# Third selective scan of a fused network kernel: units of 1024 columns on 64-row matmul tiles, with u overwritten in PSUM

## The reference

```python
def mamba_fwd(x, in_w, conv_w, conv_b, xproj_w, dt_w, dt_b, A_log, Dp, out_w):
    ...                                    # x: 4*B sequences of L = 1024, 16 channels
    xc = silu(conv(xi) + conv_b)           # di = 32 channels
    dbl = xc @ xproj_w.T                   # dt (4), B (16), C (16)
    dt = softplus(dtr @ dt_w.T + dt_b)
    A = -exp(A_log)
    def step(h, inp):
        dA = exp(dt_t[..., None] * A)
        h = dA * h + (dt_t * x_t)[..., None] * B_t[:, None, :]
        y = einsum('bds,bs->bd', h, C_t)   # 16 states
        return (h, y)
    y = ys + xc * Dp
```

## Time and profile before

| | us |
|---|---|
| median of 3 runs | 2011.63 (2010.33 to 2016.12) |
| the profiled execution | 2010.27 |
| its span in the trace | 2008.3 |
| scan3 in it, from its first instruction to its last | 1374.0 to 1904.9 |

### The profile page before, as it was taken

One profiled execution on the slowest core, in us unless ns is written; L12 is line 12 of the kernel. 1 busy time (PEld: TensorE's weight loads), 2 busy tenths in 40 slices (PEclk: granted clock), 3 DMA queues, 4 the chain that ended last, 5 costly groups with the idle time before them and its releaser, 6 DMA issues. The chain is left out here.

```text
span 2008.3 us, 31048 instructions
## 1 busy us (share of the span) xinstructions
PE 1594.7 (79%) x9878; PEld 876.8 (44%) x9878; DVE 1585.5 (79%) x1549; ACT 1164.7 (58%) x1889; POOL 1168.3 (58%) x881
## 2 busy tenths in 40 slices
PE   4888787996777877787777776667889888888787
PEld 2555434884333333333333333234555554454333
DVE  3788745554899999999999999441889999999854
ACT  3444484334666666676666665275656666665356
POOL 0666501001567676767767775202999999999701
PEclk8999988997899999899989998776999999999898
DMA  4000000000344444444444445100000000000001
GB/s 135 2 0 0 1 0 1 1 1 1 63 89 90 90 87 94 84 94 85 93 84 91 92 88 95 39 1 0 1 1 0 0 0 0 0 0 0 8 4 42
DMA packets 23435, 78.21 MB, mean 39 GB/s; under 512 B 3792, under 2 KB 4816, under 8 KB 23120
## 3 DMA queue, kind: packets, MB, share of 16 engines
q0 software_dynamic: 18432, 67.12, 17.7%
q1 hardware_dynamic: 4944, 10.35, 1.8%
HBM read 8.25 MB, written 2.10 MB: 5 GB/s over the span
## 5 line engine op out<-in xcount | busy, mean ns | idle before, releaser
L1177 POOL TENSOR_TENSOR s_prod<-s_ahead,s_cs 128x1024 f32<-128x1024 f32 x128 | 309.7, 2419 | 208.8 <-DVE s_back L1154 153.7
L1712 POOL TENSOR_TENSOR r_prod<-r_state,r_cs 128x512 f32<-128x512 f32 x256 | 323.7, 1316 | 15.7 <-DVE r_state L1653 15.1
L1151 DVE TENSOR_TENSOR_SCAN s_ahead<-s_fore,s_pfeed 128x1024 f32<-128x1024 f32 x128 | 292.7, 2287 | 10.4 <-ACT s_fore L1073 3.9
L1154 DVE TENSOR_TENSOR_SCAN s_back<-s_aft,s_pfeed 128x1024 f32<-128x1024 f32 x128 | 289.5, 2262 | 0.0
L1640 DVE TENSOR_TENSOR r_feed<-r_pu,r_bs 128x512 f32<-128x512 f32 x256 | 164.9, 689 | 64.2 <-PE r_pu L1482 64.2
L1073 ACT ACTIVATE s_fore<-s_pd,s_aneg 128x896 f32<-128x896 f32 x128 | 130.1, 1016 | 135.9 <-PE s_pd L942 135.2
L1144 DVE TENSOR_TENSOR s_pfeed<-s_pu,s_bs 128x1024 f32<-128x1024 f32 x128 | 157.8, 1233 | 35.4 <-PE s_pu L942 22.6
L1605 ACT ACTIVATE r_decay<-r_pd,r_aneg 128x512 f32<-128x512 f32 x256 | 168.7, 687 | 25.2 <-PE r_pd L1482 24.9
L942 PE MATMUL s_pu<-s_partsu,selr 64*128 64x512 f32 x512 | 102.2, 479 | 102.0 <-DVE s_pfeed L1144 102.0
L1482 PE MATMUL r_pu<-r_parts,selr 128*128 128x512 f32 x512 | 162.7, 440 | 5.7 <-DVE r_feed L1640 5.7
L1653 DVE TENSOR_TENSOR_SCAN r_state<-r_decay,r_carry,r_feed 128x512 f32<-128x512 f32 x128 | 156.5, 1267 | 0.0
(11 more groups left out here) (255 smaller groups left out, 3357.7 us busy)
## 6 DMA issues: line engine op xcount, KB each, us to landing
s_ahead<-s_back POOLq DMA_DIRECT2D x128, 512.0 KB, 4.5
x_act<-in_x_dram SPq DMA_DIRECT2D x8, 256.0 KB, 5.6
out_dram<-x_act SPq DMA_DIRECT2D x16, 128.0 KB, 2.3
k_scan<-in_pack_scan_dram SPq DMA_DIRECT2D x1, 1600.0 KB, 10.7
k_fir<-in_pack_fir_dram SPq DMA_DIRECT2D x1, 1600.0 KB, 14.0
k_l<-in_pack_l_dram SPq DMA_DIRECT2D x1, 450.0 KB, 7.1
k_ln<-in_pack_ln_dram SPq DMA_DIRECT2D x3, 131.0 KB, 2.6
k_mlp<-in_pack_mlp_dram SPq DMA_DIRECT2D x2, 194.0 KB, 5.1
```

What stands on the lines that cost most here:

```text
L1151: dve.tensor_tensor_scan(ahead[:, v % 4], f, feed[:], 0.0, ALU.mult, ALU.add).then_inc(ahead_done, 1)
L1154: dve.tensor_tensor_scan(back[:, v % 4, ::-1], a[:, ::-1], feed[:, ::-1], 0.0, ALU.mult, ALU.add).then_inc(back_done, 1)
L1177: pool.tensor_tensor(prod[:, b], ahead[:, v % 4], cs[:, buf].rearrange("p i n -> p (i n)"), ALU.mult).then_inc(prod_done, 1)
L1712: pool.tensor_tensor(prod[:, v % 2, q], state[:, v % 2, q], cs[:, v % UNROLL // 4, q], ALU.mult).then_inc(multiplied, 1)
```

## The change

`scan3` works in units: one (q, g) of 1024 columns, 128 in all, in a loop unrolled by 32 with 32 peeled ones at each end. A unit takes the place of two (q, g) of 512 columns, so the number of columns on each engine is the same.

- **u in place.** `ps_u` has two buffers of 1024 columns (two banks each), `ps_d` one, and the feed is written over `ps_u`. The separate feed banks are gone. DVE does feed, then the scan of the same unit.
- **64-row tiles.** The spread of u for one unit and of delta for the next one is one job of eight matmuls with 64 rows each, which alternate between the upper and the lower half of the array. PE waits for the scan of the unit before last, and for ACT's exp of the one before, ahead of it.
- **The scan** always starts at 0.0, as a unit holds whole sequences. The carry and its activation are gone.
- **POOL** multiplies in place in `state` (four buffers). It no longer makes `grown` (ACT does) nor the low part of B and C: PE subtracts the high part in PSUM (`negid`), and ACT copies the rest. It has six sums a group instead of eight.
- **y.** Dp * xc comes into `ps_y` by two fp32 matmuls with `place` ahead of each group of 8 units; DVE's L1669 is gone, and ACT copies `ps_y` to xc in four pieces of 32 rows.
- **First sums on VectorE.** For the first two groups, before any unit runs, the sums are DVE's (`EARLY`).
- The constants grow by `place` (512 columns) and `negid` (128), and DVE makes two tiles from them at the start.

```diff
-           ("alog", 4), ("dp", 1)],
+           ("alog", 4), ("dp", 1), ("place", 4 * P), ("negid", P)],
...
+UNROLL3, PEEL3 = 32, 32
...
-        ps_d, ps_u, feed = m.banks("r_pd", 2), m.banks("r_pu", 2), m.banks("r_feed", 2)
+        decay, state = (m.sb("r_" + t, [P, 4, 2 * N]) for t in ("decay", "state"))
+        bs, cs = (m.sb("r_" + t, [P, 2, 2, 2 * N]) for t in ("bs", "cs"))
+        ps_d, ps_u = m.banks("r_pd", 1, (P, 2 * N))[0], m.banks("r_pu", 2, (P, 2 * N))
+        ps_m, ps_y = (m.banks("r_p" + t, 1)[0] for t in "my")
...
-        LAG_B, LAG_D, LAG_U, LAG_Y = 2, 5, 6, 7
+        LAG_B, LAG_E, LAG_D, LAG_A, LAG_P, LAG_Y, LAG_V = 12, 16, 17, 18, 19, 20, 21
+        EARLY = 16
...
+        def cells(u):
+            u %= UNROLL3
+            half, phase = u // 16, u % 16 // 8
+            return half, phase, phase + u % 2 * 2, u % 8 // 2
...
         @block.tensor
+                if live(p, UNITS):              # p = s - LAG_D
+                    if (u - LAG_D) % 16 == 0:
+                        pe.wait_ge(lo_u, p + 16)
+                    wait(pe, scanned, p - 1)
+                    jobs.append((ps_u[(u - LAG_D) % 2], parts_u[:, half], q, g, u_rep))
+                if live(e, UNITS):              # e = s - LAG_E
+                    if (u - LAG_E) % 16 == 0:
+                        pe.wait_ge(lo_d, e + 16)
+                    wait(pe, decayed, e)
+                    jobs.append((ps_d, parts_d[:, half], q, g, d_ps))
+                for chunk in range(2):
+                    for part in range(2):
+                        for bank, parts, q, g, done in jobs:
+                            rows, at = slice(q // 2 * 64, q // 2 * 64 + 64), slice(chunk * N, (chunk + 1) * N)
+                            mm = pe.matmul(bank[:, at], selr[rows, (4 * q + g) * P:(4 * q + g + 1) * P],
+                                           parts[rows, part, at], start=(part == 0), stop=(part == 1),
+                                           tile_position=(q // 2 * 64, 0))
...
+                if k == 2 and live(s, UNITS):
+                    pe.wait_ge(hi_bc, gi + 8)
+                    pe.matmul(ps_m[:], negid[:], parts_bc[:, par, 0, at], start=False, stop=True,
+                              skip_group_check=True).then_inc(bc_rest, 8)
...                                             # then one spread of B or C, after s_copied, relu_done or lo_bc
+                if z % 2 == 1 and live(o, UNITS):    # o = s - LAG_Y, z = o mod 32
+                    if z % 8 == 1:
+                        wait(pe, y_done, o - 1)
+                        for chunk in range(2):
+                            pe.matmul(ps_y[:], place[:, 2 * phase + chunk],
+                                      xc[:, columns(o - z % 16 + 8 * chunk, N)], start=(chunk == 0), stop=False,
+                                      skip_group_check=True)
+                    pe.wait_ge(multiplied, o + 1)
+                    for chunk in range(2):
+                        for q in (phase, phase + 2):
+                            quad = q ^ chunk
+                            mm = pe.matmul(ps_y[quad * 32:(quad + 1) * 32], ysel[:, g * 32:(g + 1) * 32],
+                                           state[:, (z - 1 + q // 2) % 4, chunk * N:(chunk + 1) * N], start=False,
+                                           stop=(g == 3), tile_position=(0, quad * 32), skip_group_check=True)
+                    mm.then_inc(y_part, 2)
...                                             # k = 0: wdt, k = 1: wbc, both after s_copied
         @block.scalar
+                    act.wait_ge(d_ps, e + 1)
+                    wait(act, scanned, e - 3)
+                    act.activation(decay[:, v % 4], ps_d[:], ACT.Exp, scale=aneg[:, g:g + 1]).then_inc(decayed, 1)
...
+                if z % 8 == 7 and live(o, UNITS):    # o = s - LAG_V
+                    act.wait_ge(y_part, o + 1)
+                    for chunk in range(2):
+                        for q in (phase, phase + 2):
+                            rows, src = slice(q * 32, q * 32 + 32), (q ^ chunk) * 32
+                            done = act.activation(xc[rows, columns(o - z % 16 + 8 * chunk, N)], ps_y[src:src + 32],
+                                                  ACT.Copy)
+                    done.then_inc(y_done, 8)
...
         @block.vector
+                    dve.wait_ge(u_rep, p + 1)        # p = s - LAG_A
+                    if v % 8 < 2:
+                        dve.wait_ge(s_copied, p + 2 + v % 8)
+                    feed = ps_u[v % 2]
+                    dve.tensor_tensor(feed[:], feed[:], bs[:, phase, q // 2], ALU.mult).then_inc(fed, 1)
+                    dve.wait_ge(fed, p + 1)
+                    dve.wait_ge(decayed, p + 1)
+                    wait(dve, y_part, p - 3)
+                    dve.tensor_tensor_scan(state[:, v % 4], decay[:, v % 4], feed[:], 0.0, ALU.mult,
+                                           ALU.add).then_inc(scanned, 1)
...                                             # s < EARLY: three sums, du and the low parts, on DVE
         @block.gpsimd
-                    pool.tensor_scalar(grown[:], one[:], -1.0, None, ALU.add).then_inc(grown_done, 4)
-                    pool.tensor_tensor(parts[:, par, BC, 1], bcf[:], parts[:, par, BC, 0].bitcast(F32),
+                    pool.wait_ge(scanned, p + 1)     # p = s - LAG_P
+                    pool.tensor_tensor(state[:, v % 4], state[:, v % 4], cs[:, phase, q // 2],
+                                       ALU.mult).then_inc(multiplied, 1)
...                                             # k = 3: three sums, 4: du, 6 and 7: low parts
```

More of the change, by code:

```diff
@@ L1429, in _, with skewed3 @@
                 pool.tensor_tensor(resid[:, cols], out[:, cols], x[:, cols], ALU.add).then_inc(resid_done, 1)
+UNROLL3, PEEL3 = 32, 32
+def skewed3(eng, body):
+    for s in range(PEEL3):
+        body(s, s)
+    with eng.Fori(0, (UNITS - PEEL3) // UNROLL3) as r:
+        for u in range(UNROLL3):
+            body(r * UNROLL3 + (PEEL3 + u), u)
+    for s in range(UNITS, UNITS + PEEL3):
+        body(s, s % UNROLL3)
 def scan3(nc, consts, xc, selr, ysel):
@@ L1439, in scan3 @@
         c, const_in = consts["l3"]
-        wdt = m.sb("r_wdtb", [P, P])
-        delta, du, grown = m.sb("r_delta", [P, N]), m.sb("r_du", [P, N]), m.sb("r_grown", [P, N])
-        relu, ex, one, ln, bcf = (m.sb("r_" + t, [P, N]) for t in ("relu", "ex", "one", "ln", "bcf"))
-        parts = m.sb("r_parts", [P, 2, 3, 2, N], F32R)
-        decay = m.sb("r_decay", [P, 2, Q4, N])
-        state, prod = m.sb("r_state", [P, 2, Q4, N]), m.sb("r_prod", [P, 2, Q4, N])
-        carry = m.sb("r_carry", [P, Q4, Q4])
@@ L1473, in _, with scratch, columns @@
+        def scratch(s):
+            if isinstance(s, int) and 8 <= s < EARLY:
+                return state[:, 2, 0:N], state[:, 2, N:2 * N], state[:, 3, 0:N], state[:, 3, N:2 * N], decay[:, 3, 0:N]
+            return delta[:], du[:], ex[:], one[:], ln[:]
+        def columns(first, width):
+            if isinstance(first, int):
+                return slice(first * 64, first * 64 + width)
+            return ds(first * 64, width)
         @block.tensor
@@ new lines, in body @@
+                if k == 1:
+                    act.wait_ge(ex_done, gi + 8)
+                    act.activation(one, ex, ACT.Copy, bias=1.0).then_inc(one_done, 8)
+                    if isinstance(s, int) and s < EARLY:
+                        logarithm()
+                    act.wait_ge(bc_ps, gi + 8)
+                    wait(act, s_rep, gm - 16)
+                    act.activation(parts_bc[:, par, 0, at], ps_m[:], ACT.Copy).then_inc(hi_bc, 8)
+                if k == 2 and not (isinstance(s, int) and s < EARLY):
+                    logarithm()
@@ new lines, in high_d, with high_u @@
+                def high_d(group, first, delta, par, at):
+                    act.wait_ge(delta_done, group + 8)
+                    wait(act, d_ps, first - 16)
+                    act.activation(parts_d[:, par, 0, at], delta, ACT.Copy).then_inc(hi_d, 8)
+                def high_u(group, first, du, par, at):
+                    act.wait_ge(du_done, group + 8)
+                    wait(act, u_rep, first - 16)
+                    act.activation(parts_u[:, par, 0, at], du, ACT.Copy).then_inc(hi_u, 8)
```

380 lines of the change are left out of this document (165 added, 215 removed).

## The result

The changed kernel takes **1997.8 us** (median of 4, 1992.6 to 1999.5) beside 2013.9 for the kernel before (4 runs): the ratio is 0.9916, 95% interval 0.9894 to 0.9938. The forecast was 1980. The profiled execution took 1996.4 us (span 1994.6), 13.9 less than that of before, where the sum had 31.5. The time lies within the range that was given, but only about half of the gain came.

What follows compares the result with a forecast made beforehand. POOL was taken to bound the kernel before, DVE after. Terms -47.2 (DVE's pace), +2 (place), +8 (clock), +1 (start), +2.7 (end), +2 (load) sum to -31.5 from 2010.3: 1978.8, plus 1.4 for the median, 1980 us; range 1965 to 2003.

Steps and rivals of the forecast that it cites:

- POOL as the bound, and its relief: scan3: POOL sets the pace at 30.75 us a group; losing two sums and using longer products brings it to 26.8.
- DVE's pace: scan3: DVE becomes the bound at 3.48 us a unit, 445.4 against 492.6 us in all, -47.2 us.
- The feed in place: DVE's feed written over its own PSUM source: no extra cost taken, bounds 0 and 1.23 us a unit.
- Rival 2: DVE's feed in place runs at half pace, 1.23 us more a unit, kernel 2129 us; chance 0.04.
- The wait behind place: PE's y matmuls behind place, once a group: 4.7 us from a scan's end, no slack; 0.15 a group, +2 us.
- The prediction's own sign: In the trace after, DVE idle before scans, for y, once a group, means place costs more than taken.
- The clock: PE at the half clock for a tenth of the time falls 12.7 us behind a group: +8 us, bounds 0 and 25.
- Start, load, end: Around scan3's groups: start +1 us with first feed at 1407, load of larger constants +2, end after last scan +2.7.
- Rival 1: The chain through PE sets the pace at the half clock; at 0.4 of the time, kernel 2051 us; chance 0.07.
- Rival 3: POOL stays the bound, or POOL and DVE wait for each other: 28.8 us a group, kernel 1988 us; chance 0.15.
- rival 4: Nothing gained: stalls of 30 us or more from all the other rivals together, kernel 2006 to 2018 us; chance 0.05.

Runs made afterwards that it cites:

- e4: The kernel before, with only grown moved from POOL to ACT and the low part of B and C to PE and ACT: 1991.3 us, ratio 0.9880.
- e7: The changed kernel with only one of the four y copies made, three quarters of y not stored: 1981.7 us.
- e5: The changed kernel with the two place matmuls moved behind the job and spread of the next even step, nothing left out: 1976.7 us, ratio 0.9803.
- e1: The changed kernel with the two place matmuls put behind the y matmuls of the same step instead of ahead: 1989.1 us, ratio 0.9875.
- e2: The changed kernel without the two place matmuls, Dp times xc left out of y: 1970.2 us.
- e3: The changed kernel with ln and its minus one a step later on ACT: 2002.3 us.
- e12: e10 with minus one of a group made by POOL instead of ACT: 1979.8 us.
- e10: e5 with ln moved earlier on ACT, between the low-part copy of B and C and the next spread copy: 1971.0 us, ratio 0.9802.
- e6: e5 with ln and minus one of a group moved from step 2 to step 3 on ACT: 2041.4 us.

## Why the prediction was right or wrong

- **POOL as the bound, and its relief**: right. e4 shows it by itself, and after's POOL waits for scans.
- **DVE's pace**: 3.48 was 3.45, 3.8 us less in all. Right. (1.26 + 2.21 is 3.47, a slip of 1 us in all.) **The feed in place**: 1.21 us at 1024 columns, 1.23 in scan2 with two banks. Rival 2 is out.
- **The wait behind place**: this step failed. I had 2 us in all; 30.0 for y, 3.8 for decays and 1.6 for u are 35.4, less 8.1 for the clock (below) 27.3: **mis-sized by 25.3 us**. From that scan's end I had job and spread done at 1.7, the y copies at about 1.5, place 2.0 and y 1.0, together 4.7, all that DVE allows. In the usual group above, job and spread are done at 2.1, the copies only at 2.9, and place and y take 3.15: 6.1, where DVE would have been ready at 4.6. The 1.5 of lateness are 0.8 of the copies and 0.7 of the rest, and e7 agrees, where 0.4 stay without the copies. I had counted ACT's *work*, 22.4 of 27.8 us (20.5 in the trace), and not its *order*: in step 2 its copy waits for PE's spread, which waits for its copy before, and ln and minus one go ahead of the decay for which PE waits. Where I wrote "no slack" I should have gone on: with no slack every delay of a group shows in full, and what can be late there (0.8 of the copies, 0.4 of PE's job behind a late decay) is no 0.15. The prediction's own sign, DVE idle before scans, for y, once a group, came as written. e5 shows that PE's order alone decides most of it: 23.3 us hang on where two matmuls stand.
- **The clock**: 8 us against 8.1, but partly by luck: I had the half clock for a tenth of the time, 45 us, and hoped that slack would catch more than half of its 20 us. By the mean clock of the five groups that it delays (0.95, 0.95, 0.94, 0.94, 0.89) it lasts some 20 us in them, which at 12.7 us in 27.8 is 9 (an estimate), and almost none of it was caught. Two neighbouring groups, length, busy times, PEclk:

```profile
1584.06:1615.18 31.12, 24.93 (x129) 10.11 (x121) 27.39 (x17) 20.76 (x31) 26.32 (x14) 0.95 0.00 0
1615.18:1644.60 29.42, 23.30 (x129) 10.04 (x121) 27.29 (x17) 20.50 (x31) 26.28 (x14) 1.00 0.00 0
```

  Four groups are like the first, 1.1 to 1.7 us longer than the 29.5 of the others; 31.12 + 31.14 + 30.64 + 30.82 - 4 x 29.53 = 5.6. The fifth is the last group of all. From its first feed to the end of its last scan it takes 30.2 us, where that of e1, e2, e3 and e5 takes 27.65 (2.5 less): its place pair falls into a stretch at the half clock and takes 3.78 us instead of 1.98, and the scan behind it is 2.59 late.

```profile
1866.36 3.78 PE L1570 MATMUL r_py<-y_inner,r_place 128*128 128x512 f32 x4
...
1871.46 2.29 DVE L1709 TENSOR_TENSOR_SCAN r_state<-r_decay,r_pu 128x1024 f32<-128x1024 f32 x1 [2.59 <-PE r_py L1577]
```

  In the first of the five PE goes over to the half clock between these two spreads:

```profile
1589.13 0.70 PE L1560 MATMUL r_pm<-r_partsbc,selr 128*128 128x512 f32 x2 [1.47 <-ACT r_partsbc L1614]
...
1591.13 1.22 PE L1560 MATMUL r_pm<-r_partsbc,selr 128*128 128x512 f32 x2
```

  PE had idled 1.47 us before the first of them, but it does so at this point of every group (1.39 at 1620.04), so the idle time doesn't tell the one from the other.
- **Start, load, end**: +1 was -1.2 (the first feed at 1406.75, predicted 1407, and by the steps that were foreseen; the 2 us behind it were not seen, the first group takes 29.24). The load of +2: 515 KB land in 3.6 us, but scan3 starts no later; as its start differs by up to 6 us between executions, that term is not shown wrong, only not seen. End +2.7 was +2.6.
- Together: 25.3 - 3.8 (pace) + 0.1 (clock) - 2.2 (start) - 2.1 (load) - 0.1 (end) + 0.3 (behind scan3) = 17.5, and 31.5 - 13.7 is 17.8. That the time still lies in the range owes something to the terms that came out better than taken: without them it would be some 8 us longer, beyond its upper end of 2003.
- **Rival 1** named the right place, the chain from a scan's end through place to y, but put its price on the half clock. It acts at the full clock too, so a cost of its kind came without its condition. Rival 3 did not come, neither in after nor in e12; nor did rival 4, as the change gained 16 us.

Left open: what starts the stretches at the half clock (they delay five groups in after, one or two in e3, e5 and e10, nearly all in e6, and not always the same ones), what part of e4's 24 us is POOL's work, and e10's last 0.4 us of a group before y.
